# Sixteen-head attention: ones beside the values in one operand, the result turned to rows of queries, divided there and turned back

## What is computed

```
Q, K, V = x Wq, source Wk, source Wv            (source: x itself, or the context)
S[h]    = Q[h] K[h]^T / sqrt(16)                 128 x 128 for each head h = 0..15
A[h]    = softmax over keys of S[h]
y       = concat over h of (A[h] V[h])  (Wo + bo, where there is one)
x       = layernorm(x + y)
```

## Time and profile before

| | us |
|---|---|
| median of 3 runs | 2798.91 (2796.15 to 2803.93) |
| span of the profiled execution | 2795.3 |
| first scores of x1 to its last XT copy | 777.4 to 966.9 |
| first scores of x2 to its last XT copy | 1673.7 to 1844.3 |
| first scores of a3 to the last XT copy of x3 | 2111.3 to 2420.1 |

### The profile page before, as it was taken

The page is one execution under the profiler, slowest core; times in us unless marked ns, Lnnn a source line. Parts: engine busy times, 40 slices in busy tenths (PEclk is TensorE's granted clock), DMA queues, the critical chain, the costliest instruction groups (busy, mean ns, idle before and its releaser), DMA issues. The chain is left out here.

```text
span 2795.3 us, 52964 instructions
## 1 busy us (share of the span) xinstructions
PE 2395.1 (86%) x20565; PEld 1888.1 (68%) x20565; DVE 1400.2 (50%) x2861; ACT 871.3 (31%) x1510; POOL 672.0 (24%) x1002
## 2 busy tenths in 40 slices
PE   6959999668889899899979988966977879589992
PEld 3847777434578655799958866635866767379992
DVE  3256666686458631112157755753155988621114
ACT  1124333463234311011122224411234555212223
POOL 1932222241123200122212210102311222123332
PEclk9889999999999999999989989987988999789996
DMA  9020000100020000588710002013510000179994
GB/s 351 1 86 1 0 0 1 32 1 0 2 84 2 32 0 0 197 322 310 265 45 1 0 21 70 3 48 103 166 39 5 2 2 3 50 265 324 327 324 152
DMA packets 163576, 254.33 MB, mean 91 GB/s; under 512 B 17744, under 2 KB 124369, under 8 KB 163153
## 3 DMA queue, kind: packets, MB, share of 16 engines
q1 hardware_dynamic: 154192, 230.92, 24.0%
q0 software_dynamic: 9216, 21.06, 2.8%
HBM read 220.29 MB, written 31.13 MB: 90 GB/s over the span
## 5 line engine op out<-in xcount | busy, mean ns | idle before, releaser
L3236 PE MATMUL te_pU<-te_xsT,te_wu 128*128 128x128 f32 x1952 | 235.1, 278 | 1.7 <-DMA te_wg<-in_L_ffn_gate 1.0
L3236 PEld LDWEIGHTS te_pU<-te_xsT,te_wu 128*128 128x128 f32 x1952 | 232.6, 194 | 5.6 <-issue 2.5
L3257 PE MATMUL te_pY<-te_wd,te_hT 128*128 128x256 f32 x976 | 220.8, 379 | 0.0
L3257 PEld LDWEIGHTS te_pY<-te_wd,te_hT 128*128 128x128 f32 x976 | 180.7, 190 | 22.1
L1123 PE MATMUL x_pB<-early,x_xlT 128*128 128x384 f32 x384 | 135.0, 495 | 4.6 <-DVE x_qn L1350 3.0
L3277 ACT ACTIVATE te_hT<-te_pU 128x512 f32<-128x512 f32 x78 | 46.6, 597 | 242.1 <-PE te_pU L3236 242.1
L3295 DVE COPY te_ys<-te_pY 128x256 f32<-128x256 f32 x61 | 25.9, 425 | 162.8 <-PE te_pY L3257 162.8
L3290 DVE TENSOR_TENSOR te_hT<-te_pU,te_sg 128x512 f32<-128x512 f32 x44 | 30.4, 692 | 149.5 <-ACT te_sg L3275 149.5
L2292 DVE TENSOR_REDUCE x_mx<-x_pR 128x8 f32<-128x1024 f32 x64 | 78.3, 1224 | 53.1 <-PE x_pR L2076 51.3
L3275 ACT ACTIVATE te_sg<-te_pG 128x512 f32<-128x512 f32 x44 | 26.3, 597 | 251.4 <-PE te_pG L3236 251.4
L1123 PEld LDWEIGHTS x_pB<-early,x_xlT 128*128 128x128 f32 x384 | 69.8, 192 | 46.6 <-issue 3.6
(11 more groups left out here) (632 smaller groups left out, 5822.6 us busy)
## 6 DMA issues: line engine op xcount, KB each, us to landing
te_wu<-in_L_ffn_w_upT SPq DMA_DIRECT2D x39, 1024.0 KB
te_wd<-in_L_ffn_w_downT SPq DMA_DIRECT2D x39, 1024.0 KB, 5.8
te_wu<-in_L_ffn_up SPq DMA_DIRECT2D x22, 1024.0 KB
te_wg<-in_L_ffn_gate SPq DMA_DIRECT2D x22, 1024.0 KB
te_wd<-in_L_ffn_down SPq DMA_DIRECT2D x22, 1024.0 KB, 7.8
moe_first<-in_L_ffn_W SPq DMA_DIRECT2D x8, 1024.0 KB, 8.7
xs_slots<-zeros SPq DMA_DIRECT2D x1, 5120.0 KB, 23.5
ys_slots<-zeros SPq DMA_DIRECT2D x1, 5120.0 KB, 35.5
```

What stands on the lines that cost most here:

```text
L3236: ins = pe.matmul(out[g][:, m, :], w[:, k, bass.ts(PER * g + m, P)], xsT[:, k, :], start=(k == 0), stop=(k == KD - 1))
L3257: ins = pe.matmul(pY[u][:, 0, :], hT[:, k, :], wd[u][:, k, :], start=(k == 0), stop=(k == KH - 1))
```

## The change

The kernel after does the second part of each block in another way:

- The operand `V` holds 16 values and 16 ones for each head. One matmul a head (16 a block instead of 32) gives, in a strip of 32 rows, 16 rows of result and 16 rows that all hold the sum. Each head has a strip of its own, so the result is 4 x 128 columns wide instead of 2 x 2 x 128.
- ACT copies these 128 x 512 out of PSUM (`copy_output`), and four transposes (`turn_output`) put them back into the same bank, now queries by rows.
- There the sum of a head is one number a query. DVE inverts 128 x 16 numbers and multiplies 128 x 256 by them (`normalise`), into `O`, queries by features.
- For x1, x2 and x3 two transposes (`turn_normal`) and an ACT copy (`copy_normal`) give `oT` for the product with Wo. For a3 POOL adds x to `O` directly (`own_residual`), and the two transposes, POOL's copy of x and DVE's addition go.
- POOL, not ACT, puts the ready values into `V` for x2 and x3.
- The turns of every engine are written in another order. `attend` stands between the two `scores` in x2, a3 and x3 (blocks n-2), and at the turn's end in x1 (block n-1). `LAG` is gone; the pipeline has LAST + 5 turns in all three calls (before: LAST + 5 in x1 and x2, LAST + 6 in the third).
- New waits come with shared PSUM banks: in x1 `output` waits for ACT's copy of the values of block n+1; in a3 `turn_back` waits for ACT's `key(n+1)`; in x2 and x3 it waits for ACT's `query(n+1)`.

The core of the diff:

```diff
-        V = [s.sb(f"V{i}", [P, H16, ROWS]) for i in range(LAG + 2)]
+        V = [s.sb(f"V{i}", [P, H16, ROWS]) for i in range(3)]
-        R = s.sb("R", [P, KD, P])
+        oS = s.sb("oS", [P, 4, P])
+        R = s.sb("R", [P, H16])
+        O = s.sb("O", [P, D])
-        pO = s.ps("pO", [P, 2, KD, P])
+        pO = s.ps("pO", [P, 4, P])
+        back = pk[:, 0:2, :]
+        heads = pO[:].rearrange("p t (g c) -> p (t g) c", c=ROWS)
...
             for t in V:
-                pool.memset(t[:], 0.0).then_inc(v_cleared, 1)
+                pool.memset(t[:], 1.0).then_inc(v_cleared, 1)
...
+            def own_residual(b):
+                since(pool, normal, b)
+                since(pool, xn_ready, b - 1)
+                pool.tensor_tensor(r[:], O[:], core.X[:, block_of(b), :], ALU.add).then_inc(r_ready, 1)
...
-            def columns(part, lhs, b):
-                for t in range(KD):
-                    for i in range(PAIR):
-                        for g in range(P // ROWS):
-                            h = P // DH * t + PAIR * g + i
-                            ins = pe.matmul(pO[bass.ts(g, ROWS), part, t, :], lhs(h, i),
-                                            Pr[b % 2][g // NH][:, g % NH, KD * (1 - i) + t, :], start=(i == 0),
-                                            stop=(i == PAIR - 1))
+            def attend(b):
+                since(pe, v_stored, b)
+                since(pe, normal, b - 1)
+                for half in (1, 0):
+                    since(pe, w_done[half] if part(b).penalty is not None else e_done[half], b)
+                    for t in range(half, 4, 2):
+                        for c in range(P // ROWS):
+                            h = P // ROWS * t + c
+                            g, i = h % 8 // PAIR, h % PAIR
+                            ins = pe.matmul(pO[bass.ts(c, ROWS), t, :], V[b % len(V)][:, h, :],
+                                            Pr[b % 2][half][:, g % NH, KD * (1 - i) + h // 8, :], start=True, stop=True)
+                ins.then_inc(o_ready, 1)
+
+            def turn_output(b):
+                since(pe, o_copied, b)
+                for t in range(4):
+                    ins = pe.transpose(pO[:, t, :], oS[:, t, :], core.ident[:])
+                ins.then_inc(o_turned, 1)
+
+            def turn_normal(b):
+                since(pe, normal, b)
+                since_crossed(pe, oT_ready, b - 1)
+                since_crossed(pe, y_used, b - 1)
...
+                for k in range(KD):
+                    ins = pe.transpose(back[:, k, :], O[:, bass.ts(k, P)], core.ident[:])
+                ins.then_inc(back_ready, 1)
...
             for n in TURNS:                                   (PE; x2, a3 and x3)
+                before_first(n)
+                scores(n, 0)
+                if live(n - 2):
+                    attend(n - 2)
+                before_second(n)
                 scores(n, 1)
+                if crossed(n - 3):
+                    turn_normal(n - 3)
+                if live(n + 1):
+                    queries(n + 1)
+                if own(n + 1):
+                    keys(n + 1)
+                if live(n - 2):
+                    turn_output(n - 2)
+                if live(n):
+                    maxima(n)
+                if crossed(n - 3):
+                    output(n - 3)
+                if own(n - 3):
+                    turn_back(n - 3)
+                if crossed(n - 4):
+                    turn_back(n - 4)
+                if own(n + 1):
+                    value(n + 1)
...
+            def copy_output(b):
+                since(act, o_ready, b)
+                since(act, o_turned, b - 1)
+                act.copy(oS[:], pO[:]).then_inc(o_copied, 1)
...
+            def normalise(b):
+                since(dve, o_turned, b)
+                dve.reciprocal(R[:], heads[:, :, DH]).then_inc(inverted, 1)
...
+                dve.tensor_tensor(O[:].rearrange("p (h d) -> p h d", d=DH), heads[:, :, 0:DH],
+                                  R[:].unsqueeze(2).to_broadcast([P, H16, DH]), ALU.mult).then_inc(normal, 1)
```

More of the change, by code:

```diff
@@ L1868, in attention16 @@
         LAST = NB * len(parts)
-        LAG = 2 if any(p.penalty is not None for p in parts) else 1
-        TURNS = range(-1, LAST + LAG + 3)
+        OWN = NB * sum(p.own for p in parts)
+        TURNS = range(-1, LAST + 4)
         rope = parts[0].rope
@@ L1936, in live, with own, crossed @@
             return 0 <= b < LAST
+        def own(b):
+            return live(b) and part(b).own
+        def crossed(b):
+            return live(b) and not part(b).own
         def part(b):
@@ L2134, in output @@
+            def output(b):
+                since_crossed(pe, oT_ready, b)
+                if rope:
+                    since(pe, v_copied, b + 3)
+                for k in range(KD):
+                    ins = pe.matmul(y, oT[b % 2][:, k, :], part(b).early.wo[:, k, :], start=(k == 0), stop=(k == KD - 1))
                 ins.then_inc(y_ready, 1)
@@ L2253, in turn_back @@
                 since(act, xT_ready, b)
-                act.copy(core.XT[:, :, bass.ts(block_of(b), P)], pX[:, 0:KD, :]).then_inc(xT_stored, 1)
+                out = core.XT[:, :, bass.ts(block_of(b), P)]
+                act.copy(out, pX[:, 0:2, :] if rope else pk[:, 2:4, :] if part(b).own else pq[:, 2:4, :]
+                         ).then_inc(xT_stored, 1)
             for n in TURNS:
+                if rope:
+                    if live(n - 2):
+                        copy_output(n - 2)
+                    if live(n - 1):
+                        exponentials(n - 1, 1)
+                        exponentials(n - 1, 0)
+                    if live(n - 3):
+                        turn_back(n - 3)
+                    if live(n - 2):
+                        copy_normal(n - 2)
+                    if live(n + 1):
+                        query(n + 1)
+                        value(n + 1)
+                        key(n + 1)
+                    continue
@@ L2257, in _ @@
                 if live(n - 1):
                     exponentials(n - 1, 1)
-                if live(n - LAG - 3):
-                    turn_back(n - LAG - 3)
-                if rope and live(n + 1):
-                    value(n + 1)
-                if live(n + 1) and not part(n + 1).own:
-                    query(n + 1)
+                if live(n - 2):
+                    copy_output(n - 2)
+                if crossed(n + 1):
+                    key(n + 1)
                 if live(n - 1):
@@ L2266, in _ @@
                     exponentials(n - 1, 0)
[L2267 removed]
+                if crossed(n - 3):
+                    copy_normal(n - 3)
+                if live(n + 1):
                     query(n + 1)
[L2269 to L2270 removed]
+                if own(n + 1):
                     key(n + 1)
[L2272 removed]
+                if own(n - 3):
+                    turn_back(n - 3)
+                if crossed(n - 4):
+                    turn_back(n - 4)
```

285 lines of the change are left out of this document (152 added, 133 removed).

## The result

The kernel after takes 2734.76 us (median of 4 runs, 2733.32 to 2739.25) against 2797.53 (4 runs): a ratio of 0.9776, 95% interval 0.9757 to 0.9796. The span is 2731.3 against 2795.3, 64.0 us less. I forecast 2771 and a range down to 2754: the sign was right, the gain more than twice as large.

What follows compares the result with a forecast made beforehand. The prediction took PE to bound x1, x2 and x3, and DVE a3. Terms 4 + 3 + 4 + 1 + 8 + 7 = 27 us took the span from 2795.3 to 2768, the median 3.6 above: forecast 2771, 8-in-10 range 2754 to 2790.

Steps and rivals of the forecast that it cites:

- So x1, x2 and x3 go by PE: Steady turns of x1, x2, x3: PE's work sets the period, with 0.36, 0.34 and 0.44 us idle a turn.
- can't win more than its 0.34 idle: x2's turn: the gain is limited to PE's idle 0.34 us; 0.2 a turn taken, 3 us over some 14 turns.
- These go by PE and lose perhaps 1 us: a3's first four turns, 43.39 us at a clock of 0.80: PE sets their time, gain perhaps 1 us.
- Between a3 and x3: Seven turns from a3 into x3: 2.0 us less on DVE brings 61.52 to 53.5 us, 8 us, the largest term.
- a3's steady turns: Chain through ACT's key, `turn_back` and `value`: 9.58 to 9.2 us a turn, 4 us over 11 turns.
- The rival that the clock falls there: a3: the wait for ACT's key lowers the clock, 10.85 us a turn, 2789 us in all; chance 0.06.
- my loop through the keys: x1's turn: the way from `keys` to the next scores and back stays at 10.7 us, so nought for 16 turns.
- Transposes: On PE in x1, x2, x3: six more a turn at 0.15 us each, 0.9 in all, against 0.9 saved.
- The rival of 0.28: Transposes don't overlap, 0.28 us each: slower, 2817 us; chance 0.08 together with any slowdown.
- The tiling rule: PE's array drains when tiling mode changes: x3, x2 and a3 lose one of two entries, some 0.2 us each.
- Ends: Way behind the last scores of x1, x2, x3: 2, 1 and 4 us less, 7 in the sum.
- Rival (d): Whole kernel gains more: no drains, x3 7.0, a3 9.0, ends 12; 40 us, 2759 us; chance 0.18 with beyond.

Runs made afterwards that it cites:

- E6: The kernel before without the sixteen matmuls of the sums, order unchanged: ratio 1.007; x2 9.39, x3 7.93 us a turn.
- E9: The kernel before with PE turning the maxima ahead of the values' column tiles in x2 and x3: ratio 1.003; x2 9.22, x3 8.14 us a turn.
- E7: The kernel before with short reciprocal and no sums, in the old order: ratio 1.001; x2 9.40, x3 7.30 us a turn.
- E10: E7 with PE turning the maxima ahead of the values' column tiles in x2 and x3: ratio 0.995; x2 8.83, x3 6.88 us a turn.
- E14: The kernel after with its sixteen column tiles done twice: 2775.1 us, ratio 0.992.
- E5: The kernel before with DVE inverting only 128 x 16 numbers, old order and all 32 column tiles kept: ratio 0.993.
- E11: The kernel before, a3's values projected at PE's turn end and copied behind the keys: ratio 1.001; first four turns 34.7 us, steady turns 10.99.
- E2: The kernel after with a3's values projected and copied ahead of the keys again: ratio 0.986; first four turns 41.4 us, steady turns 10.30.
- E8: The kernel after with one of the four transposes in `turn_output` left: ratio 0.977; x1 10.16, a3 9.31 us a turn.
- E4: The kernel after with two unused 128 x 128 reciprocals added on DVE behind each block's product: ratio 0.999.
- E12: E2 with a3's four transposes of the result done twice: ratio 0.983; a3 9.35 us a turn.

## Why the prediction was wrong

- **"So x1, x2 and x3 go by PE" was the step that failed most.** I took busy shares of 94 to 97% for a bound and wrote that x2 "can't win more than its 0.34 idle". It won 0.7. Its period was a loop of waits, and PE's work lay in the waits' shade, as E6 and E9 show. Such a loop is not moved by PE's work (E6, E7), only by the order, and then work counts (E10, E14). In x3 too the missing sums gave nothing (E6), and the short reciprocal 0.35 (E5). x2 and x3 hold 12 of the 37 us by which the gain was missed. For x3 I had worked the new turn out, 7.0 and 7.1 by its two paths; it measures 6.76, and I had added 0.1 for drains. For x2 I had worked out none.
- **"These go by PE and lose perhaps 1 us"**, of a3's first four turns, was the largest miss for one stretch: 9.7 came. They did not go by PE, which is busy for 32.87 of the 43.39 us by the earlier trace rows itself. I had not read in the diff that `v_ready` was `q_ready` before. The split takes the values' matmuls, and with the new order their copy, out of the path from the queries to the next scores, and the clock is at 1.00 from the second turn on, where it was from the fourth (E11, E2).
- **Between a3 and x3** the mechanism was right (E5: 9.9 us come from the reciprocal alone), the size wrong: 13.2, not 8. I subtracted 1.5 us for a lower clock; it is at 1.00. The rest beyond E5 comes with the new order and the halved tiles, which are worth 3.7 there (E14).
- **a3's steady turns** came out as worked: 9.08 for 9.2, PE idle 1.54 before `turn_back`, the release from ACT's key. The rival that the clock falls there did not happen, but was near: E2, with a hole of 1.81, brought it, and in some turns so did E8.
- **x1**: 10.49 for 10.7. E5 gives 0.12 of the 0.16 to the reciprocal, which my loop through the keys left out. The first three turns won more (35.93 to 33.11) than the other twelve together (127.80 to 125.84), but x1's head lost 2.5 of it; no run separates the two.
- **Transposes**: 0.11 for 0.15. The rival of 0.28 was wrong. The error is some 0.24 us a turn for six of them, and by E8 it counts in full only in x1; in x2 and x3 a third or less of it shows, under 0.1.
- **The tiling rule** of the Trainium skill (TensorEngine Tiling, Tiling Modes, Key Properties: a change of mode drains the array) was good in kind: in a3 before, values followed by sums take 0.90 from start to start (2209.75 to 2210.65), in x3, followed by the maxima, 1.09. The sum had "small drains" of 0.1 in x3 and one in x2 for it, and even these were too much: with one entry a turn, hidden in the gap of the maxima, no drain is left to see in x3's turn after.
- **Ends**: 11.7 for 7, most of it in x3's (7.5 for 4), where the clock is 1.00 after and was 0.89. In other runs that end takes 26.7 (E5), 24.0 (E4) and 23.2 (E14), so both the reciprocal and the halved tiles have a part in it; the shares stay open.

Rival (d), "no drains, x3 at 7.0, a3 at 9.0, no lost clock in the transition", was the one that came true in its points, and even it stopped at 2759, since it had neither the loop of x2 nor a3's first turns.

## What to carry to other kernels

Before taking the fullest engine for the bound, follow one turn as a loop: if the work between two waits is taken out and the period stays, order is worth more than work. Compare the semaphores that the diff splits or joins as closely as the instructions. And in a pipeline with holes on TensorE, a hole can cost its own length and then the clock as well: read the granted clock turn by turn, for a mean over turns at two levels hides it. In E12, work put into such a hole more than paid for itself.

## What the runs showed of the hardware that I had not expected

- Work taken from TensorE can make a kernel slower: with 0.9 us a turn of matmuls left out a3 went from 9.58 to 10.22 us, the mean of eleven turns, seven near 9.58 at a granted clock of 1.00 and four of 10.4 to 12.2 at 0.72 to 0.84 (E6); 0.43 us a turn of idle repetition brought it from 10.30 to 9.35 (E12).
- In E2 the clock falls behind the hole and not in it: PE idles from 2167.07 to 2168.89 at 1.00, and 0.50 begins near 2169.7, while it works.
- Transposes of 128 x 128 f32 follow each other at 0.11 us, where each one's own length is 0.27.
